# Interleaving the first Fourier product with the layer norm, with two transpose buffers instead of four

## The reference

```python
xn = _layernorm(x, axis=-1)
x = x + attention(xn) + ffn(xn)
# attention: 16 heads of 64, softmax(q k^T / 8) v, then out @ Wo.T + bo
# ffn:
w = jax.lax.complex(w_freq_real, w_freq_imag)
x_freq = jnp.fft.fft(xn, axis=-1)
y_freq = jnp.einsum('bnd,do->bno', x_freq, w)
y = jnp.real(jnp.fft.ifft(y_freq, axis=-1)) + bias
```

## Time and profile before

| what | value |
|---|---|
| time, median of 2 runs | 4258.31 us (4206.55 to 4310.08) |
| time of the profiled execution | 4209.18 us |
| its span (slowest core, core 5) | 4207.3 us |
| spans of the eight cores | 4185.6 to 4207.3 us |
| mean granted TensorE clock of the cores | 0.849 to 0.855 |
| DMA | 231.85 MB in all, mean 55 GB/s |

### The profile page before, as it was taken

How to read it: one execution, slowest core, us unless ns; L and a number is a source line. 1 busy time by engine, 2 the same in 40 slices (tenths; PEclk the granted TensorE clock), 3 DMA queues, 4 the chain that set the end, 5 groups by cost and what they waited for, 6 DMA issues and landing times.

```text
span 4207.3 us, 48507 instructions; the slowest of 8 cores (4185.6 to 4207.3 us)
## 1 busy us (share of the span) xinstructions
PE 2670.2 (63%) x12224; PEld 882.3 (21%) x12224; DVE 2203.4 (52%) x3167; ACT 2160.5 (51%) x2146; POOL 234.5 (6%) x444
## 2 busy tenths in 40 slices
PE   1148897889666466656656665666466656656664
PEld 0123343334121111111111121112112112111111
DVE  5731133333566366636654663666366536644663
ACT  1200000000788288638855882788288648846882
POOL 1000112101000100000000001000100000010000
PEclk9998998999798689868876997899699869977996
DMA  3221133211300510160025003300610160034003
GB/s 101 74 46 20 57 136 82 47 33 68 110 1 1 137 54 1 21 170 1 1 41 150 1 1 81 110 1 1 155 36 1 26 165 1 1 62 134 1 1 75
DMA packets 95998, 231.85 MB, mean 55 GB/s; under 512 B 12736, under 2 KB 12752, under 8 KB 95744
## 3 DMA queue, kind: packets, MB, share of 16 engines
q0 software_dynamic: 45056, 111.29, 11.6%
q1 hardware_dynamic: 50688, 117.46, 9.1%
HBM read 220.32 MB, written 52.43 MB: 65 GB/s over the span
## 4 chain that ended last, share of the span: by engine, by line
ACT 24%; PE 21%; DVE 12%; DMA 10%; issue 7%; DVEq 0%; ACTq 0%; SPq 0%; POOLq 0%; POOL 0%
ACT a L902 12%; ACT xstaget L902 11%; PE pOu L807 7%; PE pSB L780 6%; DMA wo_sbt<-woT 6%; DVE rcptt L939 5%; DMA bigA<-v_scr 4%; DVE a L924 2%; ACT pt2t L902 1%; DVE zf32t L937 1%; PE pSA L877 1%; DVE a L961 1%; DVE a L958 1%; DVE scltt L929 1%; DVE a L922 1%
## 5 line engine op out<-in xcount | busy, mean ns | idle before, releaser
L902 ACT ACTIVATE a<-pSA,lnbiast 128x1024 f16<-128x1024 f32 x512 | 570.0, 1113 | 547.9 <-PE pSA L785 544.0
L924 DVE TENSOR_TENSOR a<-a 128x1024 f16<-128x1024 f16 x896 | 620.5, 693 | 319.0 <-ACT a L902 319.0
L780 PE MATMUL pSA<-a,bigB 64*128 64x512 f16 x1024 | 431.7, 422 | 555.7 <-ACT pt2t L902 393.4
L902 ACT ACTIVATE pt2t<-pSA,lnbiast 128x1024 f16<-128x1024 f32 x512 | 570.2, 1114 | 372.4 <-DVE a L922 365.4
L902 ACT ACTIVATE xstaget<-pSB,lnbiast 128x1024 f16<-128x1024 f32 x512 | 569.2, 1112 | 27.8 <-PE pSB L785 25.8
L902 ACT ACTIVATE a<-pSB,lnbiast 128x1024 f16<-128x1024 f32 x512 | 569.9, 1113 | 5.0 <-PE pSB L785 4.1
L780 PE MATMUL pSB<-a,bigB 64*128 64x512 f16 x1024 | 425.8, 416 | 197.4 <-ACT xstaget L902 100.3
L807 PE MATMUL pOu<-a,bigA 128*64 128x512 f16 x1024 | 447.5, 437 | 55.9 <-DMA bigA<-v_scr 46.2
L924 DVE TENSOR_TENSOR a<-a,pt2t 128x1024 f16<-128x1024 f16 x512 | 354.6, 693 | 221.3 <-ACT pt2t L902 221.3
L924 DVE TENSOR_TENSOR a<-a,xstaget 128x1024 f16<-128x1024 f16 x512 | 354.5, 692 | 196.0 <-ACT xstaget L902 196.0
L812 PE MATMUL pOu<-a,bigA 128*64 128x512 f16 x1024 | 449.7, 439 | 0.0
(11 more groups left out here) (141 smaller groups left out, 3486.5 us busy)
## 6 DMA issues: line engine op xcount, KB each, us to landing
bigA<-v_scr SPq DMA_DIRECT2D x256, 256.0 KB, 3.7
a<-x SPq DMA_DIRECT2D x64, 512.0 KB, 4.2
wo_sbt<-woT POOLq DMA_DIRECT2D x128, 256.0 KB, 4.5
part_scr<-a POOLq DMA_DIRECT2D x32, 512.0 KB, 2.9
a<-part_scr POOLq DMA_DIRECT2D x32, 512.0 KB, 6.6
out<-a SPq DMA_DIRECT2D x32, 512.0 KB, 4.7
q_scr<-qstaget POOLq DMA_DIRECT2D x64, 128.0 KB, 2.1
v_scr<-vstaget POOLq DMA_DIRECT2D x32, 256.0 KB, 2.4
```

What stands on the lines that cost most here:

```text
L780: te.matmul(sset[:, 0:512], KT[0:64, pr * T + kc * 128:pr * T + (kc + 1) * 128], QTs[0:64, pr * 512:(pr + 1) * 512], start=True, stop=True)
L902: AC.inc(sc.activation(PT[u % 4], SA[u % 2][:], AF.Exp, bias=lnbias, scale=0.125))
L924: DV.inc(v.tensor_add(PS[kc % 2], PS[kc % 2], PT[u % 4]))
```

## The change

The block of P0 disappears. Its matmuls are issued inside the layer-norm block: after the transposes of every fourth tile (t = 3, 7, ..., 31) PE waits for DVE's last operation of the burst before and for the loads, and runs burst a = t // 4. DVE, after the eight copies of that tile, waits for the burst's last matmul and does the same five operations, then goes on to tile t+1. POOL's loads of wr and wi wait only for the constants and, from the third on, for burst a-2. All waits on DVE's and PE's counts are renumbered (dvP, teP, dv_tile_base). Since pgr, pga and pgb take six of the eight PSUM banks, the transposes get two tiles, tp0 and tp1, in place of four, and transpose j waits for the copy of transpose j-2. The number of matmuls, copies and loads is unchanged.

```diff
-            nc.psum_tensor("tp2", [128, 128], F16) as tp2,
-            nc.psum_tensor("tp3", [128, 128], F16) as tp3,
+            nc.psum_tensor("pgr", [128, 1024], F32) as pgr,
+            nc.psum_tensor("pga", [128, 1024], F32) as pga,
+            nc.psum_tensor("pgb", [128, 1024], F32) as pgb,
...
             @blk.tensor
...
-                        if tj >= 4:
-                            tp_, jp = (tj - 4) // 8, (tj - 4) % 8
-                            te.wait_ge(semDV, dvB + tp_ * NDV + 7 + jp + 1)
+                        if tj >= 2:
+                            tp_, jp = (tj - 2) // 8, (tj - 2) % 8
+                            te.wait_ge(semDV, dv_tile_base(tp_) + 7 + jp + 1)
                         TE.inc(te.transpose(
-                            tps[j % 4][:],
+                            tps[j % 2][:],
                             xstage[:, j * 128:(j + 1) * 128], ident))
+                    teP[("tr", t)] = TE.v
+                    if t % 4 == 3:
+                        a = t // 4
+                        if a >= 1:
+                            te.wait_ge(semDV, dvP[("p0ev", a - 1)])
+                        te.wait_ge(semL[a % 2], mL1[a])
+                        for k in range(8):
...
+                            te.matmul(pgr[:, 0:512], wrs, C[0], start=st,
+                                      stop=False)
...
+                            TE.inc(te.matmul(pgb[:, 512:1024], wis, C[1],
+                                             start=st, stop=sp))
+                        teP[("p0", a)] = TE.v
...
             @blk.vector
...
                     for j in range(8):
-                        v.wait_ge(semTE, teB + t * NT1 + j + 1)
+                        v.wait_ge(semTE, teP[("tr", t)] - 8 + j + 1)
                         DV.inc(v.tensor_copy(
                             XNT[:, j * T + t * 128:j * T + (t + 1) * 128],
-                            tps[j % 4][:]))
+                            tps[j % 2][:]))
+                    assert DV.v == dvP[("tile", t)]
+                    if t % 4 == 3:
+                        a = t // 4
+                        v.wait_ge(semTE, teP[("p0", a)])
+                        DV.inc(v.tensor_copy(GrS[:, a * 1024:a * 1024 + 512],
+                                             pgr[:, 0:512]))
...
+                        DV.inc(v.tensor_copy(pstg[0], pga[:]))
+                        v.wait_ge(semDV, DV.v)
...
             @blk.gpsimd
             def _(g):
                 g.wait_ge(semIN, in_done)
-                g.wait_ge(semDV, p1a["dv"])
-                g.wait_ge(semTE, p1a["te"])
                 for a in range(8):
                     base = (a % 2) * 2048
                     if a >= 2:
-                        g.wait_ge(semTE, teB + (a - 1) * 8)
+                        g.wait_ge(semTE, teP[("p0", a - 2)])
```

More of the change, by code:

```diff
@@ L219, in build_nc @@
             mx1a[t] = _sxv[t % 2]
+        mL1 = {}
+        _lv = [c.v for c in L]
+        for a in range(8):
+            _lv[a % 2] += 32
+            mL1[a] = _lv[a % 2]
+        dvP = {}
+        _dvv = DV.v
+        for t in range(NTT):
+            _dvv += NDV
+            dvP[("tile", t)] = _dvv
+            if t % 4 == 3:
+                a = t // 4
+                _dvv += 5
+                dvP[("p0ev", a)] = _dvv
+        teP = {}
         with (
@@ L222, in build_nc, with dv_tile_base @@
             nc.psum_tensor("tp1", [128, 128], F16) as tp1,
-            nc.psum_tensor("tp2", [128, 128], F16) as tp2,
-            nc.psum_tensor("tp3", [128, 128], F16) as tp3,
+            nc.psum_tensor("pgr", [128, 1024], F32) as pgr,
+            nc.psum_tensor("pga", [128, 1024], F32) as pga,
+            nc.psum_tensor("pgb", [128, 1024], F32) as pgb,
             nc.Block() as blk,
         ):
-            tps = [tp0, tp1, tp2, tp3]
+            tps = [tp0, tp1]
             dvB, acB, teB = DV.v, AC.v, TE.v
+            def dv_tile_base(t):
+                return dvP[("tile", t)] - NDV
             @blk.tensor
@@ L240, in _ @@
                         TE.inc(te.transpose(
-                            tps[j % 4][:],
+                            tps[j % 2][:],
                             xstage[:, j * 128:(j + 1) * 128], ident))
+                    teP[("tr", t)] = TE.v
[5 more added lines that the diff above has]
+                        for k in range(8):
+                            base = (a % 2) * 2048
+                            wrs = A16[:, base + k * 128:base + (k + 1) * 128]
+                            wis = A16[:, base + 1024 + k * 128:
+                                      base + 1024 + (k + 1) * 128]
+                            C = [CSR[:, k * 1024 + h * 512:
+                                     k * 1024 + (h + 1) * 512]
+                                 for h in range(2)]
+                            S = [CSR[:, 8192 + k * 1024 + h * 512:
+                                     8192 + k * 1024 + (h + 1) * 512]
+                                 for h in range(2)]
+                            st, sp = (k == 0), (k == 7)
+                            te.matmul(pgr[:, 0:512], wrs, C[0], start=st,
+                                      stop=False)
+                            te.matmul(pgr[:, 512:1024], wrs, C[1], start=st,
+                                      stop=False)
+                            te.matmul(pga[:, 0:512], wrs, S[0], start=st,
+                                      stop=sp)
+                            te.matmul(pga[:, 512:1024], wrs, S[1], start=st,
+                                      stop=sp)
+                            te.matmul(pgr[:, 0:512], wis, S[0], start=False,
+                                      stop=sp)
+                            te.matmul(pgr[:, 512:1024], wis, S[1], start=False,
+                                      stop=sp)
+                            te.matmul(pgb[:, 0:512], wis, C[0], start=st,
+                                      stop=sp)
+                            TE.inc(te.matmul(pgb[:, 512:1024], wis, C[1],
+                                             start=st, stop=sp))
+                        teP[("p0", a)] = TE.v
@@ L292, in _ @@
                     assert sX[t % 2].v == mx1a[t]
[L294 to L358, removed]
@@ L377, in _ @@
                     assert L[a % 2].v == mL1[a]
+        p1a = dict(dv=DV.v, te=TE.v, ac=AC.v)
+        if phases < 2:
+            _final(nc, [(semIN, IN.v), (semX0, sX[0].v), (semX1, sX[1].v)])
+            return nc
         p0s1 = dict(dv=DV.v, te=TE.v)
```

22 lines of the change are left out of this document (17 added, 5 removed).

## The result

The changed kernel is slower by 1.05%: the ratio of its time to that of the kernel before is 1.0105, 95% interval 1.0073 to 1.0137. Medians: 4258.77 us (17 runs) against 4212.46 us (15 runs). The profiled execution has a span of 4239.2 us, 31.9 more than before.

A forecast was written before the change was run, and what follows sets the result against it. Bound by a sequence of stages, with PE and DVE in series in layer norm and P0; -14.9 + 38.7 + 2.0 = +25.8 us on 4209.2 gave 4235 us, range 4195 to 4285.

The forecast's parts named there:

- the sum: Whole kernel: all predicted gains and costs together, +25.8 us on the profiled 4209.18 us, given as 4235 us.
- everything later shifted by the same amount: Stages behind the second Fourier product: they only start later, with attention still taking 3207 us within 15.
- Terms 1 and 2: Layer norm and P0: P0's own stage goes (-173.2 us), its eight bursts return in the layer-norm chain (+158.3): -14.9 us.
- Term 3: Layer-norm transposes: two buffers instead of four need four rounds of 0.74 us, +1.21 us a tile, +38.7 us.
- The first rival: Layer-norm transposes: fewer buffers cost nothing, PE and DVE find slack or the round is shorter; 4196 us, chance 0.10.
- Term 4: Start of the kernel: POOL's four casting loads beside SP's load of x0 cost +2 us, bounds 0 and +8.5.
- The clock: P0's bursts on PE: each already pays for a low clock, so interleaving costs nothing more, 0 us.
- The price of the slow part: P0's bursts: matmuls at low clock cost 2.7 us of each burst's 15.89 us.
- the third rival: P0's bursts: spreading them adds seven cold starts of 2.7 us, +19 us, 4254 us; chance 0.03.
- The last rival: Attention: its granted clock falls from 0.82 to 0.75, PE's part grows by 82 us, to 4317 us; chance 0.03.

The follow-up runs named there:

- its own experiment: Kernel before with its first four loads of wr and wi issued at the start of layer norm; one profiled run, 4211 us, stretch 392.7 us against 400.2.

## Why the prediction failed, point by point

**Two steps failed.** The first is the base of the sum. The sum was +25.8 us on an execution of 4209.2 us, and 4235 was given as the time. Against the median shown then, 4258.31 us, that number reads as a gain, and the text left it so: it knew that the median lay 49 us above its base and only widened the range upwards. The change is a loss, of 32 us between the profiled executions, 35 in the mean of their cores and 44 by the ratio. So the sign of the sum was right and the number given was not the sum's statement about the change; it should have been 25.8 us above whatever the kernel before measures.

The second is a term put at nothing: "everything later shifted by the same amount". Up to the second Fourier product the sum was nearly right, 25.8 us against 20.5 on core 5 and 22.4 in the mean of the cores. Behind it the runs show 11.4 us more on core 5 and 12.6 in the mean, for which the sum had no term (below, "What the sum left out"). That the measured median, 4258.77, lies in the stated range is no merit of the sum, since the range had been widened for a median of 4258.31 that was itself too high.

**Terms 1 and 2, -14.9.** Right within 2 us. With four buffers the stretch is 16.9 us shorter on core 5 and 15.3 in the mean. The load wait is 7.5 of it, by its own experiment.

**Term 3, +38.7.** Right, in mechanism and size. The round of 0.74 us, four rounds, the first sum at 2.86 us (2.87 measured) and the tile of 8.2 us (8.18) all came out, and the buffers alone cost 36.8 us of the stretch and 39.6 in the whole. The first rival, that the ring costs nothing, is refuted.

**Term 4, +2.** Too high. The first sum starts at 31.20 us where it started at 31.77. DVE had waited 5.20 us for x0 and 4.92 before; from the issue of the load to the sum it is 4.92 us (26.28 to 31.20) where it was 4.64 (27.13 to 31.77), so the four loads beside it cost 0.3 us.

**The clock, 0.** Nearly right. The price of the slow part was read too high: a fast step takes 0.216 us (five steps from 426.16 to 427.24 in the kernel before) and not 10.9 / 52 = 0.21, which leaves 2.3 us a burst and not 2.7. The bursts of core 5 take 14.7 to 16.3 us, together 123.6 us, against 127.1 before, first to last matmul start, because five to thirteen of their steps are slow and not nine to thirteen. The transposes right before a burst seem to help now and then: 3.5 us for the eight, of the 18 that full speed from the start would have saved. That the reason is the transposes was not tested. No cold starts came on top, so the third rival is out. The Trainium skill, TensorE: Matmul & The Clock Gate, in its part on the clock gate, says that the clock falls to half in idle time. The trace agrees in both kernels: the old bursts start at 0.50 after a pause of 4.5 us, and these are two windows of the changed kernel, with PEclk in the third last column:

```profile
85.00:117.00 32.00, 6.37 (x33) 3.40 (x34) 19.23 (x59) 5.97 (x12) 0.00 (x0) 0.50 0.26 73
...
123.00:133.00 10.00, 10.00 (x48) 4.51 (x46) 0.00 (x0) 0.00 (x0) 0.00 (x0) 1.00 0.01 2
```

PE has the level of 1.2 GHz through four tiles of layer norm, with transposes alone, and 2.4 GHz inside the burst. The way the clock is recorded also explains why the mean granted clock of the cores fell from about 0.85 to 0.825 with no matmul slower for it: before, the 220 us of layer norm were shown as 1.00, since the first entry of the clock in that trace is at 272.7 us, though its transposes ran at the same 0.13 us pitch as here.

**What the sum left out.** "Everything later shifted by the same amount" was wrong. Of the 12.6 us in the mean of the cores 7.5 lie in attention. That part is shown: it is the one late place a pair of heads, which the removed block brought about by shifting the lists (9.1 us by the medians, 7.6 when the block is put back). The last rival had put the danger in attention as well, but in its clock; the granted clock there is 0.83 in both kernels, and this rival is out. Another 5 us lie in the projections and before, which differ by as much between kernels that share that code (405.7 to 415.1 us in the mean of the cores from the q projection to the first exponential); what makes them differ stays open. The 9 to 12 us by which the ratio of 1.0105 exceeds the difference of the profiled executions need no stage of their own: the one profiled here, 4241.03 us, is the second fastest of the changed kernel's 17 runs.

## What to carry to other kernels

Before two stages are interleaved, look at where each in-order queue waits: work placed behind a wait for the other engine is not beside it. The stretch of 400 us went to 421 with the waits at the burst and fewer buffers, and to 252 with the bursts cut to the length of the work beside them, the wait moved one tile on, and two wide hand-overs a tile instead of eight. Price a ring of buffers by its round (0.74 us here between PE and DVE) times the number of rounds, make the buffers wide where banks are short, and state what is predicted as a difference from the base.

## What the runs showed of the hardware

ACT has a place in its instruction list where the next instruction comes late with nothing to wait for, one in each of the 64 pairs of heads. That is once every 32 exponentials, or every 128 instructions in this loop (three waits and one operation each; the trace has 8438 rows on ACT for 2048 exponentials and 96 other activations). In the kernel before it takes 1132 ns instead of 1005, behind key tile 17; with two instructions fewer ahead of it 1274 ns at the same tile, 9 us in all; with two more 1274 ns one tile earlier. A packet of 8192 bytes of instructions is loaded within 1.4 us of it in 92% of the cases. The Trainium skill, Runtime: NRT & Kernel Launch, in its section on instruction fetch mechanics, says that instructions are refilled in blocks of 256 and that the cost of a boundary is mostly hidden. The distance seen here is half of that, and up to 0.27 us of it is not hidden. That the boundary of such a block is the cause fits all of this and was not tested by itself; the position was.
